# Attention over 1024 keys on one core: the unread transposes ahead of each weighted head are taken out of the loop

## The reference, cut to what matters

```
q, k, v: 16 heads of 16 values, rounded to 8-bit steps (k and q by row, v by column)
attn = softmax(q @ k.T)              # 1024 queries x 1024 keys, for each of 16 heads
attn = round(attn / (rowmax/255)) * (rowmax/255)
out  = attn @ v ; out @ Wp + bp
```

## Time and profile before

| | |
|---|---|
| median of three runs | 332.67 us (331.87 to 333.02) |
| the profiled execution | 335.32 us |
| its span, first to last instruction | 333.3 us |
| mean granted TensorE clock | 0.873 |
| busy | PE 222.8 us, PEld 154.3, DVE 266.8, ACT 199.7, POOL 171.7 |

### The profile page before, as it was taken

How to read it: one execution, slowest core, us unless ns; L and a number is a source line. 1 busy time by engine, 2 the same in 40 slices (tenths; PEclk the granted TensorE clock), 3 DMA queues, 4 the chain that set the end, 5 groups by cost and what they waited for, 6 DMA issues and landing times.

```text
span 333.3 us, 6118 instructions
## 1 busy us (share of the span) xinstructions
PE 222.8 (67%) x2126; PEld 154.3 (46%) x2156; DVE 266.8 (80%) x399; ACT 199.7 (60%) x335; POOL 171.7 (52%) x291
## 2 busy tenths in 40 slices
PE   4891498595324764767767677776777767678670
PEld 4440266483112551045555455554545545457560
DVE  3552799959689799879999899999989999983850
ACT  1100125345344135789999999999989999893210
POOL 2360324457783430255566565565555656554634
PEclk9998559878555595579999999999999999999998
DMA  7825000019960007979988889889889988995011
GB/s 258 277 95 127 0 1 2 0 22 190 169 126 0 0 0 144 174 140 160 142 163 149 121 174 161 140 168 149 144 151 150 160 129 174 144 135 105 16 48 63
DMA packets 131694, 38.95 MB, mean 117 GB/s; under 512 B 126288, under 2 KB 130768, under 8 KB 131664
## 3 DMA queue, kind: packets, MB, share of 16 engines
q1 hardware_dynamic: 129568, 35.14, 59.6%
q0 software_dynamic: 768, 2.10, 1.8%
q10 hardware_dynamic: 1328, 1.32, 1.2%
HBM read 5.25 MB, written 2.10 MB: 22 GB/s over the span
## 4 chain that ended last, share of the span: by engine, by line
issue 31%; POOL 27%; DVE 20%; PE 11%; DMA 6%; ACT 4%; POOLq 0%; ACTq 0%; DVEq 0%
POOL gates L456 14%; POOL ebias L448 7%; PE ps L1081 4%; DMA ksplit<-in_x 3%; PE ps L1192 3%; POOL scratch L386 2%; POOL rstd L392 2%; DMA xs<-scratch 2%; DVE hs L887 2%; DVE nmax L921 1%; DVE stats L893 1%; ACT ctxT L609 1%; POOL out L484 1%; ACT ctx L609 1%; PE ps L1184 1%
## 5 line engine op out<-in xcount | busy, mean ns | idle before, releaser
L921 DVE TENSOR_REDUCE nmax<-ps 128x1 f32<-128x1024 f32 x128 | 153.1, 1222 | 10.0 <-PE ps L1210 8.2
L1210 PE MATMUL ps<-keysT,kv 128*128 128x512 bf16 x226 | 75.3, 408 | 48.3 <-ACT ctx L609 25.3
L609 ACT ACTIVATE ctx<-ps,ebias,qscale 128x1024 uint8<-128x1024 f32 x64 | 76.6, 1199 | 7.9 <-POOL ebias L448 7.0
L609 ACT ACTIVATE ctxT<-ps,ebias,qscale 128x1024 uint8<-128x1024 f32 x64 | 76.6, 1199 | 4.9 <-POOL ebias L448 4.1
L448 POOL TENSOR_SCALAR ebias<-nmax,qscale 128x1 f32<-128x1 f32 x128 | 33.9, 264 | 75.4 <-DVE nmax L921 68.3
L456 POOL CAST gates<-ksplit 128x1024 int16<-128x1024 uint8 x64 | 66.3, 1036 | 10.2 <-DMA ksplit<-ctx 3.6
L1234 PEld LDWEIGHTS ps<-identb 128*128 128x128 bf16 x484 | 37.3, 98 | 29.0 <-issue 1.1
L1234 PE MATMUL ps<-identb 128*128 128x128 bf16 x484 | 47.3, 221 | 0.3 <-POOL gates L456 0.3
L1210 PEld LDWEIGHTS ps<-keysT,kv 128*128 128x128 bf16 x256 | 15.1, 99 | 60.6 <-ACT ctx L609 27.7
L515 ACT COPY hT<-ps 128x256 f32<-128x256 f32 x11 | 4.1, 372 | 48.2 <-PE ps L1073 48.1
L1241 PE MATMUL ps<-vals,gates 128*128 128x16 f16 x512 | 22.4, 170 | 0.0
(11 more groups left out here) (180 smaller groups left out, 348.5 us busy)
## 6 DMA issues: line engine op xcount, KB each, us to landing
ctx<-in_ctx SPq DMA_DIRECT2D x2, 512.0 KB, 5.0
ksplit<-in_x ACTq DMA_DIRECT2D x1, 1024.0 KB, 10.9
xs<-scratch SPq DMA_DIRECT2D x1, 1024.0 KB, 5.6
wkv_s<-in_L_xattn_Wkv SPq DMA_DIRECT2D x1, 512.0 KB, 8.0
ksplit<-ctx SPq DMA_TRANSPOSE x32, 3.8
ksplit<-ctxT SPq DMA_TRANSPOSE x32, 3.7
bkv_b<-in_L_xattn_bkv ACTq DMA_DIRECT2D x1, 256.0 KB, 11.3
wt_s<-in_L_ffn_weight SPq DMA_DIRECT2D x1, 256.0 KB, 9.4
```

Source lines behind the costliest of these rows:

```text
L609: a.activation(probs, s_in, ACT.Exp, bias=ebias[:, u % 4:u % 4 + 1], scale=qscale[:, t, u:u + 1], accum_out=lsum[:, t, u:u + 1]).then_inc( ...
L921: v.tensor_reduce(nmax[:, u % 4:u % 4 + 1], score_banks(k, u), AX.X, ALU.max, negate=True).then_inc(max_ready, 1)
L1210: last = m.matmul(ps[:, bank + b, :], qT[:, t, u // 2, :], keysT[:, u % 2, u // 2, 512 * b:512 * b + 512], start=True, stop=True)
```

## The change

The four transposes ahead of the eight matmuls of a weighing are taken out, with the constant and the argument that chose them. Nothing else moves: not the waits, not the order, not the lag of seven heads, and the keys' operand keeps its 128 rows with the zeros in 64 of them.

```
-FILLERS = 4
...
-            def weigh(t, k, u, fillers=True):
+            def weigh(t, k, u):
...
-                if fillers:
-                    idle = ps[:, PV_BANKS[k % NS], D:2 * D].bitcast(BF16)
-                    for i in range(FILLERS):
-                        m.transpose(idle[:, i * P:(i + 1) * P], identb[:, :], identb[:, :])
                 out = ps[:, PV_BANKS[k % NS], u * HD:(u + 1) * HD]
...
-                weigh(NT - 1, NT - 1, u, fillers=False)
+                weigh(NT - 1, NT - 1, u)
```

## The result

The kernel after took 342.9 us (median of four runs, 340.88 to 343.42) against 332.85 us for the kernel before (331.87 to 334.68): a ratio of 1.0284, 95% interval 1.0223 to 1.0345. (The ratios here are worked out from the single runs, so they are not quotients of the medians.) Taking 484 transposes out made it slower by 10 us. The forecast was 345.3 us in a range of 334.5 to 351.

A forecast was written before the change was run, and what follows sets the result against it. VectorE's maximum and ScalarE's exponential, nearly without pause, and the three-buffer score ring were taken as bounds. Loop +11.4, start -0.5, divisions -0.3, behind the loop +2.0 gave +12.6 on 332.67: 345.3 us, range 334.5 to 351.

The forecast's parts named there:

- The ring: Attention loop: scores, maximum, bias and exponential must close within three heads; 1.26 us a head at 2.4 GHz, 1.37 at 1.2.
- The clock falls: Attention loop: without transposes TensorE pauses in each head, so four fifths of the loop runs at 1.2 GHz, costing 11.4 us.
- The price of a head at 1.2 GHz: Attention loop: each of 119 heads affected costs 0.12 us more at the low clock, bounds 0.11 and 0.14.
- The divisions: Seven divisions where VectorE waits for the weighing: 0.22 us less each, at most 1.5 us; a fifth taken, -0.3 us.
- The start of weighing: First weighings at 1.2 GHz: two groups of transposes of 0.43 us go; gain 0 to 0.86, taken as 0.5 us.
- Behind the loop: Dense fp32 transposes and matmuls after the loop start at the low clock: +2.0 us, bounds 0 and 3.5.
- The sum: Whole kernel: 11.4 - 0.5 - 0.3 + 2.0 = +12.6 us, giving 345.3 us, 3.8% slower.
- signs named ahead: Profile after: mean clock about 0.6 to 0.7, heads three apart 4.0 to 4.2 us, VectorE idle before the maximum 15 or more.
- A: Loop: clock stays up and the transposes' time is gained at divisions and start, -2.0 us, 330.7 us; chance 0.10.
- B: Loop: clock stays up but ring and VectorE give back the gain at each division, 332.7 us; chance 0.06.
- C: Loop: clock goes up and down, three tenths at 1.2 GHz, +3.3 us, 336.0 us; chance 0.17.
- D: Loop: TensorE becomes the bound at 1.2 GHz, heads at 1.5 us, 357 us; chance 0.05.

The follow-up runs named there:

- e9: Kernel before, with four transposes also behind the scores of the first seven heads: 333.62 us, ratio 0.9997.
- e1: Kernel before, with two transposes ahead of each weighing instead of four: 334.35 us, ratio 1.0021.
- e2: Kernel before with its four transposes, the first score matmul of each head issued twice: 338.79 us, ratio 1.0157.
- e3: Kernel before without transposes, the first score matmul of each head issued twice: 337.57 us, ratio 1.0111.
- e6: Kernel before without transposes, the first score matmul of each head issued three times: 344.48 us, ratio 1.0305.
- e8: Kernel before, its four transposes left out for the last head of each tile alone: 333.43 us, ratio 0.9974.
- e10: Kernel before, with transposes added in the first seven heads and none for the last head of a tile: 331.59 us, ratio 0.994.
- e11: Like e10, plus eight transposes in place of the scores the last three heads lack and eight more behind them: 331.14 us, ratio 0.991 against the kernel before.

## Why the prediction was right, step by step

**The ring.** Right, and shown by one and by two extra score matmuls with the clock at 1.00 in the loop (+5.1 and +9.5 us). Not all of a longer latency comes through: 0.04 us a head where a third of 0.21 is 0.07. Why stays open. Of the chain of work that ended last in the loop before (205 to 295 us), GpSimd's unpacking has 28% and its bias 13%, and no run changed these.

**The clock falls.** Right in that it fell and stayed mostly low: 0.68 of the loop against the four fifths taken. The reason given was incomplete in two ways. It read pauses of TensorE from the rows, but in the loop of the kernel with 64-row scores and transposes TensorE never paused and the clock never rose. The 128 rows of the operand are part of the story, and no row of before could show it. And its main evidence, that scores alone had not raised the clock in the first heads, did not hold every time: in the profile after they did, at 134 us, behind the same six matmuls. That the clock fell again at once there is what the forecast needed, and it had no row for it but the two falls at 64 and 81 us.

**The price of a head at 1.2 GHz.** This is the term that was most mis-sized: 0.12 us taken, with bounds of 0.11 and 0.14. Measured are 7.0 / (0.68 x 116) = 0.089 in the kernel after, and 0.091 in the loop all at 1.2 GHz; both lie below the low end. It came from the ring alone, three heads against three heads. Over the whole loop a head took 1.31 us at the high level and 1.40 at the low one, each longer than its ring (1.26 and 1.37), and the difference of these means is what counts. So the loop was 7.0 and not 11.4 us; of the 4.4 us between them the share (0.68 for 0.8) makes 1.7 and the price nearly all the rest.

**The divisions.** -0.3 forecast. Their wait went from 3.2 us to 2.4:

```profile
DVE krest L959 <- PE ps L1236: 2.4, 7, 0.6
```

What the loop had of these 0.8 us is inside the 7.0 and can't be told apart.

**The start of weighing.** -0.5 forecast, 0.0 measured. From the first to the twelfth exponential took 15.1 to 16.6 us over the profiles of all kernels here, so one profile each can't tell a term of this size. No run took it apart; e9, with the clock up in part of the same heads, changed nothing measurable either.

**Behind the loop.** +2.0 forecast, +2.5 measured. The kernel after ran its first dense work there at 1.2 GHz until 311.5 us. But 1.5 of the 2.5 us is not the change's alone: five of the kernels with a clock held in nearly all of the loop (e1, e2, e3, e6, e8) took 33.9 us there, with a short fall at the end of the loop, and before, e9, e10 and e11 took 32.4 without one. That the term fits so well is in part luck.

**The sum.** Forecast +12.6 in the median, measured +10.05; the terms in the profiles give 7.0 + 0.0 + 2.5 = 9.5. Two of the signs named ahead fell a little short, as a smaller share and price make them: the mean clock is 0.717 and not 0.6 to 0.7, and VectorE's idle time in front of the maximum 13.6 us and not 15 or more.

**The rivals.** A and B fell with the clock line. The rule of the Trainium skill behind A ("TensorE: Matmul & The Clock Gate", "Part 4: PE-mode transpose": transposes don't count as busy in the way of a matmul) is not borne out here: 1, 2 and 4 transposes a head took the low share of the loop from 0.68 to 0.26, 0.02 and 0, and one more score matmul, with as many columns as four transposes, took it to 0.02. C had the right picture, a clock that goes up and down, and the wrong share. D did not come in the kernel after, but did where the clock was low and the transposes stayed: 1.71 us a head, 381.4 us.

## What to carry to other kernels

Work on an idle engine can be worth its place for the clock it holds. The price of losing that clock was paid here in latency, not in throughput: look for the ring of buffers through which the engine's result must come back. Before taking such work out, find where the trace shows the engine doing only what would be left, and read the clock there, in more than one profile: a single one said that scores alone don't raise it, and the next said otherwise. And take out what stands on the path first: here that was one group of transposes in sixteen, whose wait became 1.6 us shorter (the run with that edit alone could not be told from no change), while to take all of them out cost 7 in the loop.

## What was not expected of the hardware

Score matmuls over 64 rows, with the transposes, left the clock at 1.2 GHz for 225 us, of which TensorE was busy 216.76:

```profile
126.00:351.00 225.00, 216.76 (x1727) 106.68 (x1725) 162.09 (x149) 167.66 (x260) 99.28 (x191) 0.50 0.68 121
```
The same matmuls over 128 rows, half of them zeros in the keys' operand, left it at 2.4 GHz from 146 us to the end of the loop and beyond. With the transposes in both, the zeros were worth 47.5 us (381.4 against 333.9): the low clock, and TensorE as the bound at it. Without the transposes in either, the loop with 64 rows was at 1.2 GHz all through, the one with 128 rows for 0.68 of it.
